# An attention layer with six-bit feed-forward: two PSUM banks for scores, five for maxima and pieces

## What is computed

```python
x = x + attention(layernorm(x), Wq, Wk, Wv, Wo, bo)   # 16 heads of 16, causal, scores / sqrt(256)
x = x + mx_linear(layernorm(x), weight, bias)
```

## Time and profile before

| | |
|---|---|
| median of 3 runs | 2093.06 us (2091.07 to 2094.66) |
| the profiled execution | 2085.36 us |
| its span, first to last instruction | 2083.6 us |
| PE busy | 1980.0 us (95%) |
| PE weight loads | 755.4 us (36%) |
| DVE busy | 1716.6 us (82%) |
| ACT busy | 1351.9 us (65%) |
| POOL busy | 810.7 us (39%) |
| 16 DMA engines, mean | 27% |
| mean granted TensorE clock | 0.987 of 2.4 GHz |

### The profile page before, as it was taken

How to read it: one execution, slowest core, us unless ns; L and a number is a source line. 1 busy time by engine, 2 the same in 40 slices (tenths; PEclk the granted TensorE clock), 3 DMA queues, 4 the chain that set the end, 5 groups by cost and what they waited for, 6 DMA issues and landing times.

```text
span 2083.6 us, 35416 instructions
## 1 busy us (share of the span) xinstructions
PE 1980.0 (95%) x11749; PEld 755.4 (36%) x11749; DVE 1716.6 (82%) x4358; ACT 1351.9 (65%) x2881; POOL 810.7 (39%) x1123
## 2 busy tenths in 40 slices
PE   6799899999999999999999999999999999999984
PEld 3333333333333343434334343433333433333433
DVE  4797886869887978796897879797889899888875
ACT  5357566767766767676766666666766666677661
POOL 3323414231335554553243646453345444211232
PEclk9999999999999999999999999999999999999997
DMA  4442221414041241703323161340614121130000
GB/s 155 123 111 64 77 68 38 102 48 120 9 123 55 74 99 38 174 11 81 93 53 95 46 140 50 79 102 17 160 39 112 54 55 40 39 90 24 9 31 21
DMA packets 162963, 152.04 MB, mean 73 GB/s; under 512 B 32982, under 2 KB 150492, under 8 KB 162780
## 3 DMA queue, kind: packets, MB, share of 16 engines
q1 hardware_dynamic: 162780, 149.77, 27.0%
HBM read 91.89 MB, written 57.02 MB: 71 GB/s over the span
## 4 chain that ended last, share of the span: by engine, by line
PE 71%; DVE 19%; ACT 3%; issue 3%; POOL 2%; SPq 2%; DMA 1%; POOLq 0%; ACTq 0%; DVEq 0%
PE psum L1496 20%; PE psum L1479 19%; PE psum L1464 16%; DVE max_parts L1201 8%; PE psum L1560 8%; PE psum L1553 5%; DVE psum L1196 4%; ACT probs L1005 2%; SPq L674 1%; PE psum L1531 1%; DVE max_parts L1196 1%; ACT acc_sb L1014 1%; PE psum L1582 1%; PE psum L1523 1%; DVE stats L1259 1%
## 5 line engine op out<-in xcount | busy, mean ns | idle before, releaser
L1005 ACT ACTIVATE probs<-psum 128x512 f32<-128x512 f32 (+3 forms) x2560 | 1211.6, 536 | 518.9 <-PE psum L1479 511.8
L1201 DVE TENSOR_REDUCE max_parts<-psum 128x1 f32<-128x512 f32 x1536 | 965.2, 682 | 123.6 <-PE psum L1464 119.5
L1479 PE MATMUL psum<-q_rows,k_rows 99*128 99x512 bf16 (+3 forms) x2560 | 856.1, 351 | 3.3 <-ACT probs L1005 1.9
L1464 PE MATMUL psum<-k_rows,q_rows 96*128 96x512 bf16 (+3 forms) x2560 | 815.7, 349 | 30.2 <-DVE max_parts L1201 11.4
L1496 PE MATMUL psum<-probs,v_in 128*17 128x512 f32 (+3 forms) x5120 | 594.3, 536 | 11.9 <-ACT acc_sb L1014 11.5
L1196 DVE CUSTOM_DVE_ANT_0 psum<-psum,causal 128x128 f32<-128x128 f32 (+3 forms) x1024 | 476.5, 518 | 135.5 <-PE psum L1464 132.7
L1479 PEld LDWEIGHTS psum<-q_rows,k_rows 99*128 99x128 bf16 x2560 | 237.2, 97 | 640.5 <-ACT probs L1005 500.3
L833 POOL TENSOR_SCALAR_AFFINE_SELECT probs<-probs 128x512 f32<-128x512 f32 x256 | 165.9, 648 | 727.3 <-ACT probs L1005 727.1
L1464 PEld LDWEIGHTS psum<-k_rows,q_rows 96*128 96x128 bf16 x2560 | 244.6, 98 | 291.7 <-DVE max_parts L1201 81.8
L1496 PEld LDWEIGHTS psum<-probs,v_in 128*17 128x17 f32 x5120 | 86.1, 95 | 226.7 <-issue 162.1
L1196 DVE DVE_READ_ACCUMULATOR2_ANT max_parts<- 128x1 f32 x1024 | 144.9, 141 | 0.0
(11 more groups left out here) (161 smaller groups left out, 1268.7 us busy)
## 6 DMA issues: line engine op xcount, KB each, us to landing
q_rows<-qk_scratch SPq DMA_DIRECT2D x384, 64.0 KB, 2.7
k_rows<-qk_scratch SPq DMA_DIRECT2D x384, 64.0 KB, 2.7
qk_scratch<-shop SPq DMA_DIRECT2D x56, 384.0 KB, 3.2
sums_scratch<-acc_sb SPq DMA_DIRECT2D x48, 256.0 KB, 2.3
shop<-in_L_attn_x SPq DMA_DIRECT2D x19, 512.0 KB, 5.2
v_scratch<-shop SPq DMA_DIRECT2D x16, 544.0 KB, 4.3
v_in<-v_scratch SPq DMA_DIRECT2D x64, 136.0 KB, 2.6
out_shop<-in_L_attn_x SPq DMA_DIRECT2D x12, 512.0 KB, 8.5
```

Source lines behind the costliest of these rows:

```text
L1005: nc.scalar.activation(probs[s % NPROBS][:, h, a:CHUNK], bank[SCORE_BANKS[n % 3]][:, a:CHUNK], ACT.Exp, scale=SCALE).then_inc(probs_ready, 1)
L1201: nc.vector.tensor_reduce(max_parts[k % 2][:, first:first + heads, t % TILES, c], ring_bank(UNIT_USE[n])[:, 0:heads * width] .rearrange("p ...
L1464: ins = nc.tensor.matmul(dst[:, i * width:(i + 1) * width], q_rows[u][0:ROWS, qc, first + i, t % TILES * P:(t % TILES + 1) * P], k_rows[u] ...
L1479: nc.tensor.matmul(bank[SCORE_BANKS[n % 3]][:, a:CHUNK], k_rows[u][0:ROWS + LEVELS, h, kb * P:(kb + 1) * P], q_rows[u][0:ROWS + LEVELS, qc ...
```

## The change

The banks for scores become two, the accumulator and the ring move down, and the ring gets a fifth bank. The score's bank and both of its users go by n % 2, and PE waits for Exp n - 2 in place of Exp n - 3. `RING = len(RING_BANKS)` follows, and with it every `emptied` and `ring_bank`. The planner is not changed, so the order of all work on every engine stays as it is.

```diff
@@ -373,7 +373,7 @@
-SCORE_BANKS, ACC_BANK, RING_BANKS = [0, 1, 2], 3, [4, 5, 6, 7]
+SCORE_BANKS, ACC_BANK, RING_BANKS = [0, 1], 2, [3, 4, 5, 6, 7]
 RING = len(RING_BANKS)
@@ -1002,7 +1002,7 @@
                 act.wait_ge(scores_ready, n + 1)
-                nc.scalar.activation(probs[s % NPROBS][:, h, a:CHUNK], bank[SCORE_BANKS[n % 3]][:, a:CHUNK], ACT.Exp,
+                nc.scalar.activation(probs[s % NPROBS][:, h, a:CHUNK], bank[SCORE_BANKS[n % 2]][:, a:CHUNK], ACT.Exp,
                                      scale=SCALE).then_inc(probs_ready, 1)
@@ -1475,8 +1475,8 @@
-                wait(pe, probs_ready, n - 2)
-                nc.tensor.matmul(bank[SCORE_BANKS[n % 3]][:, a:CHUNK],
+                wait(pe, probs_ready, n - 1)
+                nc.tensor.matmul(bank[SCORE_BANKS[n % 2]][:, a:CHUNK],
                                  k_rows[u][0:ROWS + LEVELS, h, kb * P:(kb + 1) * P],
```

## The result

The changed kernel takes 2164.63 us (median of 4 runs, 2163.23 to 2165.95) against 2093.15 us before: ratio 1.0349, 95% interval 1.0334 to 1.0365. That is 71.5 us more; the forecast was 2176 us, range 2142 to 2220. The profiled execution took 2164.33 us around a span of 2162.6 us, which is 79.0 us more than the profiled span of before. The two differences do not agree because the profiled execution of before was itself 7.7 us under its median. The quotient of the medians is 1.0342; the recorded ratio takes in every run, the profiled ones too.

A forecast was written before the change was run, and what follows sets the result against it. PE's own in-order instruction list was taken to bound the attention loop. Score waits +121 us less 38 us given back made +83, carried to the median: 2093 + 83 = 2176 us, range 2142 to 2220.

The forecast's parts named there:

- The price of a slot: Slots without an item: score 0 0.20 us late, 0.25 in all with four pieces; 0.47 with few pieces.
- The gross cost of 121 us: Attention loop, score waits: 316 full slots 79 us, 77 short slots 36, item slots some 6.
- The prediction's own rule: Pieces' weight loads: each can go one matmul, 0.22 us, ahead; of 110 us waiting about 54 is PE time.
- What is given back: Ring waits of PE's pieces: fifth bank and longer slots together return 38 us, some 70% of the 54.
- The ends: Before 100 us and after 2035 us: no scores or waits for data, so no change.
- the +83 of the sum: Whole kernel: +121 - 38 = +83 us, carried from the profiled execution to the median, giving 2176 us.
- DVE was the limit all along: Rival: pieces wait for DVE in most slots, so score waits fall in lost time; +32, 2125 us, chance 0.07.
- The bank is free before the Exp's record ends: Rival: score bank released at the Exp's pitch, 0.49 us; -11, 2082 us, chance 0.03.
- The clock falls: Rival: small PE gaps drop the loop's clock to 0.91; 1850 us take 10% more, 2361 us, chance 0.03.
- The Trainium skill's budget for an Exp: Rule beside the forecast: 0.725 us per 512-wide Exp, score 0 0.33 late, 104 us on 316 slots; not used.
- The signs named: PE share falls, idle before scores grows to many tens, full slot 3.08 us, attend or projection slots and other engines unchanged.

The follow-up runs named there:

- the wait alone: Kernel before, three score banks and ring of four, with only the wait changed to the Exp two back: 2176.96 us, ratio 1.0417.
- part (a) alone: Changed kernel with two score banks but a ring of four, one bank idle: 2178.48 us, ratio 1.0427 to the kernel before.
- the two kernels with a ring of three: Kernel before with its ring cut to three: 2167.43 us, ratio 1.0385; changed kernel with its ring cut to three: 2235.68 us, ratio 1.0705.
- early pieces: Changed kernel with PE's pieces of a slot dealt 2, 1, 1, 0 behind scores 0 to 3: 2192.09 us, ratio 1.0495.

## Why the prediction was right

- **The price of a slot** (0.20 and 0.25 us late, 0.47 with few pieces) was right to 0.01 us in the slots shown. Its parts were each in the trace: start to Exp, length of the Exp, pitch, release. This is the mechanism, and the experiments leave no other: the wait alone costs the same as two banks, and the cost moves with the distance and with the length of the Exp.
- **The gross cost of 121 us.** The lengthened slots add up to 123.9 us in the change and to 121.0 with a ring of four. That the total fits so well is partly luck, since the parts do not. The prediction gave all 316 full slots the 0.25 us of the one shown; they lengthened by 63.2 us in place of 79, for in only 153 of them was score 0 at 0.88 us before. The 77 short slots lengthened by 42.4 us in place of 36, and the rest, mostly slots with an item, by 18 in place of 6. A slot can hold a new score wait and a saved ring wait at once, so these sums are lower bounds on the two effects. The prediction's own rule leads to the same place: in part (a) alone the loads of the pieces wait 44.5 us in 102 waits; with 0.22 us of each hidden, 22 us is PE's, against 54 before, so 32 us came back, and with the ratio of 1.0427, or 89 us, the gross cost is 121 us. No run tested the 0.22 us.
- **What is given back** was sized at 38 us. By the same rule 21.9 us in 53 waits leave 10 us in the change, so 44 us came back, of which 32 without the fifth bank. The shortened slots add up to 42.0 us, and to 28.5 with a ring of four. The term was sized low, by 4 to 6 us.
- **The ends.** "No change" ahead of the first score was not quite right: it comes 3.4 us earlier. How much of this is the fifth bank is not settled: the other kernels with a ring of five have it at 91.1 to 93.5 us, those with a ring of four at 92.7 to 94.3.
- **The time itself.** The net of the loop by the profiles is 81.9 us, against the +83 of the sum; the medians are 71.5 us apart. The prediction carried its sum from the span to the median of before, and that median lies 7.7 us above the profiled execution, where the profiled execution of after is at its median. This is 7 of the 11 us between 2176 and 2164.63; the other 4 are the sum itself, 83 against 79.0.
- **The rivals.** *DVE was the limit all along*: the two kernels with a ring of three show that banks do count, but the change lies far above its 2125 us, so most slots were not held by DVE. *The bank is free before the Exp's record ends*: excluded, since in the profile of the change no score starts less than 0.055 us behind the end of the Exp two back, and 798 of them start within 0.075 us. *The clock falls*: mean 0.987 in both profiles. (The loop from first to last score is 1939 us long and not 1850, which matters for this rival's price alone.) The Trainium skill's budget for an Exp ("ScalarE: Activation LUTs", "Rules for kernel authors"), 0.725 us for 512 columns, would have put score 0 at 1.21; the trace has 1.08. But the page gives this budget for an instruction whose bias is a [128,1] pointer operand, and the Exp at L1005 is given no bias. So the prediction held a budget against the trace that was not for this Exp, and the difference of 0.12 us does not speak against the page.
- **The signs named.** The idle time ahead of the scores did not grow to "many tens" on PE's own rows; it is 18.1 us for ACT there, and the wait stands with the weight loads (782.3 us). A full slot took 3.09 us, as named. The slots with an item did not keep their length but got shorter. DVE and POOL kept their busy times within 13 us; ACT's grew by 30, since its Exps follow one another less closely and so overlap less (1107.88: three in a row, where there were four). PE's busy time grew with the span, 1980.0 to 2052.8 us, and its share stayed at 95%. There the prediction read the view wrongly: records of matmuls 0.38 us long bridge gaps of up to 0.16 us between starts 0.22 us apart, so most of the new wait looks busy. With early pieces, where score 0 is 0.42 us late, the row shows 0.25 us idle ahead of it, and PE's share falls to 92%.

## What to carry to other kernels

With two buffers between two engines, ask for the distance in the producer's list from one use to the next but one, and compare it with matmul to start, plus the consumer's whole record, plus release (here 0.42 + 0.60 + 0.06 = 1.08 us). Averages do not decide this: ACT was busy 65%, and the values left ample time in the middle of each slot, but the score pairs at the slot boundary had only 0.88. And a deeper ring is worth less wherever another wait slows its producer: the fourth bank was worth 80 us to the kernel before and 58 to the one with the score wait. The fifth, tried with the score wait alone, was worth 16.

## What the runs showed of the hardware that was not expected

In the profiled run with three score banks and a ring of three the mean granted clock is 0.977, against 0.987 in the profiled run of before. Eleven stretches inside its loop, 51 us in all, run at the 1.2 GHz level, ten of them behind places where PE waited for ring banks. The kernel before has three such stretches in its loop, 10 us in all, and the change four, 14 us; two of each also follow a wait for a ring bank (of 2.09 and 0.83 us before, 0.94 and 1.95 in the change). Stretches of the kernel with a ring of three (length, busy us of PE, PEld, DVE, ACT and POOL, clock, DMA share, GB/s):

```profile
618.00:623.00 5.00, 4.13 (x22) 1.11 (x21) 5.00 (x9) 3.70 (x8) 2.43 (x6) 1.00 0.73 172
623.00:630.00 7.00, 6.19 (x22) 1.99 (x21) 5.27 (x10) 2.56 (x7) 0.64 (x1) 0.51 0.46 132
630.00:635.00 5.00, 4.85 (x34) 1.76 (x34) 2.95 (x15) 3.52 (x9) 0.44 (x1) 1.00 0.56 137
```

The wait for a ring bank as this stretch begins, and the values of a slot in it and of one behind it:

```profile
623.90 0.61 PE L1464 MATMUL psum<-k_rows,q_rows 96*128 96x512 bf16 x1 [0.81 <-DVE max_parts L1201]
...
625.18 1.91 PE L1496 MATMUL psum<-probs,v_in 128*17 128x512 f32 x8
...
630.20 1.05 PE L1496 MATMUL psum<-probs,v_in 128*17 128x512 f32 x8
```

The eight passes take 1.91 us at the lower level and 1.05 at the upper. By the means, (1 - 0.977) x 2 x 2172 = 100 us of this span were at the lower level, against (1 - 0.987) x 2 x 2083.6 = 54 us before. PE does about half the work in them, so as an estimate up to 23 us of that run may be the clock. But it is the run with the lowest clock: the other three have 0.980 to 0.983, and the kernel before on the same chip 0.981 to 0.985. From the medians of these, 0.981 and 0.984, the same working gives some 8 of the 80 us. It was not tried apart. The rival of the falling clock was thus no empty one. The rule of the Trainium skill that stood beside it ("TensorE: Matmul & The Clock Gate", "A second HAM failure mode: psum-queue depth-cycling") has its counterpart in this kernel, in a small way. In the change, whose waits are more but shorter (0.2 to 0.5 us a slot), the mean clock is 0.987 and no lower than before.
